# Pacing the second run of first-layer experts beside the first run and the selective scan

## The chip, the cores and the metric

The kernel runs on one core of a Trainium2 chip. The metric is the device time of one execution in microseconds; of several executions the median is given. A core has a matrix engine (TensorE, PE in the rows, its weight loads PEld), a vector engine (VectorE, DVE), an activation engine (ScalarE, ACT), a general engine (GpSimd, POOL) and SyncE (SP), which issues transfers. Each takes its own instructions in program order, and they are tied by semaphores only.

## The reference

Six blocks act in turn on x, of 8 sequences x 512 tokens x 128 features. The first three are the stage that the change touches:

```python
x = x + 0.5 * _L0_ffn_ref(_layernorm(x), W_gate, W1, b1, W2, b2)   # first run of the experts
x = x + _L0_attn_ref(_layernorm(x), ...)                           # a Mamba layer: selective scan
x = x + 0.5 * _L0_ffn_ref(_layernorm(x), ...)                      # second run, same weights
x = x + 0.5 * _L1_ffn_ref(...)                                     # the other three blocks
x = x + _L1_attn_ref(...)
x = x + 0.5 * _L1_ffn_ref(...)

def _L0_ffn_ref(x, W_gate, W1, b1, W2, b2):        # D=128, E=8 experts, H=512, top 2 by a mask
    gate = einsum('bsd,de->bse', x, W_gate)
    kth = top_k(gate, 2)[0][..., -1:]
    mask = softmax(where(gate >= kth, gate, -inf))
    h = relu(einsum('bsd,edh->bseh', x, W1) + b1)
    y = einsum('bseh,ehd->bsed', h, W2) + b2
    return (y * mask[..., None]).mean(axis=-2)

def step(h, inp):                                  # the selective scan, 256 channels x 16 states
    dA = exp(dt_t[..., None] * A)
    h = dA * h + (dt_t * u_t)[..., None] * B_t[:, None, :]
    y = einsum('bdn,bn->bd', h, C_t)
```

Every expert is computed for every token, and the mask weights the results.

## The kernel before

The function `front` computes the first three blocks of all eight sequences as three streams of work that run side by side: `A`, the first run of the experts; `M`, the Mamba layer; `F`, the second run. A sequence must leave `A` before `M` takes it and leave `M` before `F` takes it. The remaining 796 us of the kernel (attention and the experts of the second layer) come behind `front` and are not touched.

**Steps.** A run of the experts has 256 steps: 8 sequences x 8 experts x 4 chunks of 128 hidden features. One step is three matmuls of 512 columns for the up product (lines 118 to 120, the weights and the input being split in a high and a low part), a relu on ACT (line 385, out of one PSUM bank into `hf0`, `hf1` or `hf2`), and the down product for the four token tiles of the step two before (line 354). Behind every fourth step VectorE adds the expert's result, weighted by the mask, onto x (line 413, four instructions). While a sequence is worked on, the norm, the gate and the mask of the next are made in between, at fixed places of its 32 steps (lines 74 to 325). Names that end in `a` belong to the first run, in `b` to the second.

**Scans.** The Mamba layer also has 256 steps, 32 for a sequence (16 states x 2 halves of the channels). One is a decay on ACT (line 767, into `bank4` or `bank5`), a product on POOL (line 777), the scan itself on DVE (line 782), a second product on DVE (line 797) and a sum on POOL (line 808). The projections, the convolution and the softplus of the next sequence stand between them at fixed places (`PREP_*`; lines 612, 620, 626 on PE, 699 to 710 on DVE), and so do the gate and the output projection of the one before (`TAIL_*`; 717 to 728 on PE, 739 and 745 on ACT, 752 and 758 on DVE, 595 and 598 on POOL).

**Slots.** What interleaves the streams is `weave`. It counts slots, and in every slot it takes from each stream so many steps, on each engine alike, as the stream's pace says (one, where it has none). `M` has its scan number 0 in slot 56 (`LM`), one in each slot, and its last in slot 311; its tail lasts until slot 322. `A` begins in slot -12 with 12 steps of preparation and has a pace of its own:

```python
def pace(slot):
    if slot < LM:
        return 1 + (LM - 27 <= slot < LM - 25)
    return 1 + (slot % 3 != 0) if slot < LB else int(slot % 5 != 0)
```

From slot 56 to 109 it takes five steps in three slots, from slot 110 (`LB`) on four in five; its last expert step falls in slot 245. `F` begins in slot 98 with 12 steps of preparation, so that its first expert step falls in slot 110, and takes one step in each slot: its last falls in slot 365. The norms of the block behind `front` are woven in from slot `LN` on, one sequence in five slots (`norms_dve`, `norms_act`).

**Banks.** `HB` and `YB` are two PSUM banks each, for the up and the down products. While both runs are live, each has one of the two; a run that is alone uses both by turns. `first` and `second` decide it by the slot in which the step falls.

Of the kernel before, what the change touches and what calls it, by code (L numbers as in the profile page):

```python
# [17 lines left out]
E = 8  # L18
HID = 512
HC = HID // P  # L20
# [149 lines left out]
def weave(*parts):  # L170

    slot, live = min(part[0] for part in parts), list(parts)
    while live:
        for part in list(live):
            steps = part[2](slot) if len(part) > 2 else 1
            if slot >= part[0] and any(next(part[1], "end") == "end" for _ in range(steps)):
                live.remove(part)
        slot += 1
# [680 lines left out]
def front(nc, S, C, bank, lasting, xin, a, f0, K, w1, sorted_rows):  # L859

    NJ, LM, LB = E * HC, 56, 110
    END = NSEQ * NJ
    LN, norms = LB + END - 40, K["norms"][0]

    def pace(slot):
        if slot < LM:

            return 1 + (LM - 27 <= slot < LM - 25)  # L870
        return 1 + (slot % 3 != 0) if slot < LB else int(slot % 5 != 0)

    with ExitStack() as ctx, ExitStack() as scan_ctx:
        def sb(name, shape, dt=F32):
# [6 lines left out]
        HB, YB, DH, XB, XM = B[0:2], B[2:4], bank[4:6], B[6], B[7]  # L881
# [8 lines left out]


        slots_of_first = [slot for slot in range(-12, 2 * END) for _ in range(pace(slot))]

        def slot_of_first(v):
            return slots_of_first[v + 12]


        def first(k, until):
            return k % 2 if slot_of_first(until) <= LB else 0

        def second(k, since):
            return k % 2 if since >= slot_of_first(END + 2) else 1


        M = mamba(S, C, sb_scan, a, x_of, lambda s: A["done"](s), x_of, lambda s: M["x_read"](s), rows_dram, DH, XM)
# [6 lines left out]
        zero_row, zeroed, cleared = sb("zero_row", [P, NT, WIDE]), S.count("k_zero_row"), S.dma("k_rows_cleared", E * TILES // NT)  # L912
        W = ffn0_up(nc, S, sb, f0)
        A = ffn0(S, C, sb, W, "a", x_of, loaded, x_of, loaded, lambda J: first(J, J + 1), lambda G: first(G, 4 * G + 6), HB, YB, XB)
        F = ffn0(S, C, sb, W, "b", x_of, M["done"], x_of, M["done"], lambda J: second(J, LB + J), lambda G: second(G, LB + 4 * G), HB, YB, XB)

        W["raw"] = F["spent"]
        raw_ld, split = [S.dma(f"k_raw{r}_loaded", (E + 1) * NU // 2) for r in range(4)], K["split"]
# [33 lines left out]
        def split_experts(eng):  # L952
            W["pool"](eng)
            yield

        def pool(eng):
            eng.memset(zero_row[:], 0.0).then_inc(zeroed.sem)
            weave((-12, A["pool"](eng), pace), (0, split_experts(eng)), (LM - NJ, M["pool"](eng)), (LB - 12, F["pool"](eng)))
            eng.wait_ge(*M["done"](NSEQ - 1))
            for i, e in enumerate([E] + list(range(E))):  # L960
                for u in range(NU):
                    k, hi, lo = NU * i + u, K["up_hi"][u][:, e, :], K["up_lo"][u][:, e, :]
                    eng.wait_ge(raw_ld[k % 4].sem, raw_ld[k % 4].at(k // 4))
                    eng.tensor_copy(hi, A["spent"][k % 4]).then_inc(split.sem)
                    eng.wait_ge(split.sem, split.at(k, "hi"))
                    eng.tensor_tensor(lo, A["spent"][k % 4], hi.bitcast(F32), ALU.subtract).then_inc(split.sem)


        def norms_dve(eng):
            for s in range(NSEQ - 1):  # L970
                eng.wait_ge(*F["done"](s))
                norms.mean(eng, s)
                yield
                yield
                norms.scale(eng, s)
                yield
                yield
                yield

        def norms_act(eng):  # L980
            for s in range(NSEQ - 1):
                yield
                norms.root(eng, s)
                for _ in range(4):
                    yield

        def act(eng):
            weave((-12, A["act"](eng), pace), (LM - NJ, M["act"](eng)), (LB - 12, F["act"](eng)), (LN, norms_act(eng)))

        def dve(eng):  # L990
            eng.memset(W["b2"][:], 0.0).then_inc(W["b2_zero"].sem)
            eng.wait_ge(W["b1_T"].sem, W["b1_T"].at(0))
            eng.tensor_copy(W["b1"][:].rearrange("p e c -> p (e c)"), XB.psum[:, 0:E * HC]).then_inc(W["b1_at"].sem)
            weave((-12, A["dve"](eng), pace), (LM - NJ, M["dve"](eng)), (LB - 12, F["dve"](eng)), (LN, norms_dve(eng)))

        def pe(eng):
            eng.wait_ge(W["small"].sem, W["small"].at(0, "b1"))
            eng.transpose(XB.psum[:, 0:E * HC], W["b1_rows"][:], C["ident"][0:E * HC, 0:E * HC]).then_inc(W["b1_T"].sem)
            XB.free = (W["b1_at"].sem, W["b1_at"].at(0))
            weave((-12, A["pe"](eng), pace), (LM - NJ, M["pe"](eng)), (LB - 12, F["pe"](eng)))  # L1000

        with nc.Block() as block:
            block.sync(sync)
# [1138 lines left out]
```

## Time and profile before

| | us |
|---|---|
| median of 3 runs | 1939.84 |
| the runs | 1930.39, 1939.84, 1942.37 |
| profiled execution, its own time | 1927.48 |
| its span, first to last instruction | 1925.7 |
| busy: PE | 1752.5 (91%) |
| busy: DVE | 1250.3 (65%) |
| busy: POOL | 1210.9 (63%) |
| busy: ACT | 1103.0 (57%) |

The span is the time from the first instruction to the last; the 1.8 us to the execution's own time lie around it. Busy times are sums over the whole kernel. Matmuls overlap in the array and their ends are modelled, so that a PE that is busy for 95% of a stretch has hardly anything left to give there. The share of an engine over the whole span says little here, since the streams overlap differently from stage to stage; the windows below cut the stage at the slots at which a pace changes.

### The profile page before, as it was taken

What the parts mean: (1) busy time and instruction counts of PE and PEld (TensorE: products, weight loads), DVE (VectorE), ACT (ScalarE), POOL (GpSimd) and SP (SyncE); (2) the same over time, 40 slices, a digit from 0 to 9 for tenths busy, and PEclk for the clock granted to TensorE, in tenths of its full rate; (3) what the DMA queues carried; (4) which work ended last, traced back from release to release, by engine and by line L of the source; (5) the groups of instructions that cost most, each with busy time, mean ns of one, the idle gap of its engine ahead of it and who ended that gap; (6) DMA issues with size and microseconds to landing.
All of it is one profiled execution on the core that took longest, in us unless ns stands there. A gap on an engine that the chain in (4) does not pass through costs nothing. (4 is left out here: it accounts for less than half of the span.)

```text
span 1925.7 us, 35660 instructions
## 1 busy us (share of the span) xinstructions
PE 1752.5 (91%) x12117; PEld 1506.5 (78%) x12117; DVE 1250.3 (65%) x2930; ACT 1103.0 (57%) x1935; POOL 1210.9 (63%) x1201
## 2 busy tenths in 40 slices
PE   7999898999999999887689989999699999989998
PEld 6878676787877778766477878888599999978886
DVE  2358789778787787978886436433567666656433
ACT  3466665766666766565555554343577767553442
POOL 3228687776877768778895725464656555534664
PEclk9999999999999999999889989999799999989999
DMA  4023332332333223332221401112554354101113
GB/s 145 1 69 113 92 107 87 108 97 86 102 91 109 94 84 108 91 101 78 78 99 55 117 14 44 38 46 67 156 160 127 116 154 137 39 24 35 46 45 108
DMA packets 120638, 166.95 MB, mean 87 GB/s; under 512 B 13878, under 2 KB 55820, under 8 KB 120460
## 3 DMA queue, kind: packets, MB, share of 16 engines
q1 hardware_dynamic: 112716, 147.74, 25.2%
q0 software_dynamic: 7168, 15.87, 2.7%
q8 instruction: 101, 1.65, 0.3%
q10 hardware_dynamic: 576, 1.05, 0.2%
q14 instruction: 77, 0.63, 0.1%
HBM read 114.28 MB, written 50.33 MB: 85 GB/s over the span
## 5 line engine op out<-in xcount | busy, mean ns | idle before, releaser
L777 POOL TENSOR_TENSOR db<-du_m,bt 128x512 f32<-128x512 f32 x256 | 328.5, 1284 | 137.6 <-DVE bank L782 136.7
L782 DVE TENSOR_TENSOR_SCAN bank<-bank,db 128x512 f32<-128x512 f32 x256 | 312.5, 1221 | 20.1 <-ACT bank L767 19.9
L808 POOL TENSOR_TENSOR y_m<-y_m,ph 128x512 f32<-128x512 f32 x240 | 313.4, 1307 | 0.4 <-DVE ph L797 0.4
L767 ACT ACTIVATE bank<-dt_m,a_neg 128x512 f32<-128x512 f32 x256 | 176.2, 688 | 96.6 <-DVE ph L797 90.0
L797 DVE TENSOR_TENSOR ph<-bank,ct 128x512 f32<-128x512 f32 x240 | 165.9, 691 | 11.2 <-POOL y_m L808 3.2
L1241 POOL TENSOR_TENSOR s_a<-s_a,mx_a 128x768 f32<-128x768 f32 x64 | 94.2, 1472 | 88.3 <-DVE mx_a L1349 88.2
L1380 PE MATMUL bank<-vb_a,pT_a 96*128 96x64 f32 x1024 | 121.5, 272 | 0.2 <-DVE o_a L1391 0.2
L1380 PEld LDWEIGHTS bank<-vb_a,pT_a 96*128 96x128 f32 x1024 | 119.4, 192 | 0.3 <-DVE o_a L1391 0.3
L354 PEld LDWEIGHTS bank<-dn,hf2b 128*128 128x128 f32 x680 | 91.3, 196 | 15.4 <-DVE x_all L413 5.7
L354 PEld LDWEIGHTS bank<-dn,hf1b 128*128 128x128 f32 x680 | 89.8, 193 | 11.2 <-DVE x_all L413 2.9
L354 PE MATMUL bank<-dn,hf2b 128*128 128x128 f32 x680 | 92.1, 280 | 6.5 <-DVE x_all L413 4.7
L354 PEld LDWEIGHTS bank<-dn,hf0b 128*128 128x128 f32 x688 | 90.3, 192 | 9.3 <-DVE x_all L413 1.0
L354 PEld LDWEIGHTS bank<-dn,hf2a 128*128 128x128 f32 x680 | 89.6, 193 | 8.5 <-DVE x_all L413 1.3
L354 PEld LDWEIGHTS bank<-dn,hf0a 128*128 128x128 f32 x688 | 90.3, 192 | 7.5
L354 PEld LDWEIGHTS bank<-dn,hf1a 128*128 128x128 f32 x680 | 89.0, 191 | 8.0 <-DVE x_all L413 0.6
L354 PE MATMUL bank<-dn,hf1b 128*128 128x128 f32 x680 | 90.7, 277 | 2.4 <-DVE x_all L413 2.0
L354 PE MATMUL bank<-dn,hf0b 128*128 128x128 f32 x688 | 91.1, 275 | 1.0 <-DVE x_all L413 0.6
L354 PE MATMUL bank<-dn,hf0a 128*128 128x128 f32 x688 | 90.8, 275 | 0.0
L354 PE MATMUL bank<-dn,hf2a 128*128 128x128 f32 x680 | 90.4, 276 | 0.4 <-DVE x_all L413 0.3
L354 PE MATMUL bank<-dn,hf1a 128*128 128x128 f32 x680 | 89.7, 275 | 0.2 <-DVE x_all L413 0.2
L385 ACT ACTIVATE hf1a<-bank,b 128x512 f32<-128x512 f32 x85 | 58.2, 685 | 53.6 <-PE bank L120 53.3
L1311 ACT CAST qd_a<-q_strips_a 32x512 fp32r<-32x512 f32 x128 | 78.7, 615 | 15.6 <-DMA q_strips_a<-q_rows 14.5
(458 smaller groups left out, 4864.9 us busy)
## 6 DMA issues: line engine op xcount, KB each, us to landing
bt<-bc_rows SPq DMA_DIRECT2D x128, 256.0 KB, 3.5
ct<-bc_rows SPq DMA_DIRECT2D x128, 256.0 KB, 3.4
sorted<-zero_row SPq DMA_DIRECT2D x64, 288.0 KB, 3.9
k_strips_a<-k_rows SPq DMA_DIRECT2D x32, 256.0 KB, 3.0
q_strips_a<-q_rows SPq DMA_DIRECT2D x32, 256.0 KB, 3.9
q_rows<-q_hi_a SPq DMA_DIRECT2D x16, 256.0 KB, 3.0
q_rows<-q_lo_a SPq DMA_DIRECT2D x16, 256.0 KB, 3.4
vb_a<-v_rows SPq DMA_DIRECT2D x16, 240.0 KB, 3.9
```

The costliest lines, as they stand in the source:

```text
L354: x = eng.matmul(Y.psum[:, t], hf[r][:, t], W["dn"][:, e, c, :], start=c == 0 and k == 0, stop=c == HC - 1 and k == NT - 1, skip_group_che ...
L385: eng.activation(hf[v % NR][:], HB[hbank(v)].psum[:], ACT.Relu, bias=W["b1"][:, e, c:c + 1]).then_inc(relu.sem)
L767: eng.activation(DH[J % 2][:], dt[s % 2][:, j % NH, :], ACT.Exp, scale=a_neg[:, j % NH, j // NH:j // NH + 1]).then_inc(da_done.sem)
L777: eng.tensor_tensor(db[J % RD][:], du[s % 2][:, j % NH, :], bt[N % RB][:], ALU.mult).then_inc(db_done.sem)
L782: eng.tensor_tensor_scan(DH[J % 2][:], DH[J % 2][:], db[J % RD][:], 0.0, ALU.mult, ALU.add).then_inc(hs_done.sem)
L797: eng.tensor_tensor(out, DH[J % 2][:], ct[N % RB][:], ALU.mult).then_inc(ph_done.sem)
L808: eng.tensor_tensor(y[s % 2][:, j % NH, :], y[s % 2][:, j % NH, :], ph[J % RP][:], ALU.add).then_inc(ys_done.sem)
L1241: eng.tensor_tensor(X[:], X[:], M[:, :, None].to_broadcast([P, UB, KW]), ALU.subtract).then_inc(sub_done.sem)
L1311: x = eng.copy(qd[n % RQ][p, :, r, :], q_strips[n % 2][p, :].rearrange("p (b q) -> p b q", q=QB))
L1380: x = eng.matmul(BO[:, at:at + 2 * GD], pT[u % 2][:, c * BB + j, :], vb[s % 2][:, b:NB + 1:NB - b, g * GD:(g + 1) * GD], start=True, stop= ...
```

## The change

`F` gets a pace. It begins in slot 95 instead of 98, takes four steps in five slots until slot 249 (those slots whose number leaves 2 when divided by 5 are left out, whereas `A` leaves out those that leave 0), then four steps in three slots until slot 326, and one in each slot from there on. The functions that choose its banks ask for the slot by the new table. The norms for the block behind begin in slot 318 instead of 326. No instruction is added, removed or resized in any engine's list but two loads of activation tables on ACT (40 where there were 38); the streams are only dealt out otherwise.

```diff
-    NJ, LM, LB = E * HC, 56, 110
+    NJ, LM, LB, LA, L2 = E * HC, 56, 110, 249, 95
     END = NSEQ * NJ
-    LN, norms = LB + END - 40, K["norms"][0]
+    LN, norms = LB + END - 48, K["norms"][0]
...
+    def pace_second(slot):
+        if slot < LA:
+            return int(slot % 5 != 2)
+        return 1 + (slot % 3 == 0) if slot < LM + END + 14 else 1
...
+        slots_of_second = [slot for slot in range(L2, 2 * END) for _ in range(pace_second(slot))]
+
         def slot_of_first(v):
             return slots_of_first[v + 12]
+
+        def slot_of_second(v):
+            return slots_of_second[v + 12]
...
-        F = ffn0(S, C, sb, W, "b", x_of, M["done"], x_of, M["done"], lambda J: second(J, LB + J), lambda G: second(G, LB + 4 * G), HB, YB, XB)
+        F = ffn0(S, C, sb, W, "b", x_of, M["done"], x_of, M["done"], lambda J: second(J, slot_of_second(J)), lambda G: second(G, slot_of_second(4 * G)), HB, YB, XB)
...
-            weave((-12, A["pe"](eng), pace), (LM - NJ, M["pe"](eng)), (LB - 12, F["pe"](eng)))
+            weave((-12, A["pe"](eng), pace), (LM - NJ, M["pe"](eng)), (L2, F["pe"](eng), pace_second))
```

The same edit of the last line stands in the functions of the other engines. Counted by the two tables, the steps of `F` fall thus (those of `A` and the scans stay where they are):

| slots | scans | steps of `A` | steps of `F` before | steps of `F` now |
|---|---|---|---|---|
| 110 to 245 | 136 | 108 | 136 | 109 |
| 246 to 311 | 66 | 0 | 66 | 86 |
| 312 and on | 0 | 0 | 54 | 61 |

How it looks on ACT, where a slot begins with its decay (line 767) and the relus of the two runs follow. This is the stage with both runs live, a part of it without preparations, before:

```order
L767 ACTIVATE bank5<-dt1_m,a_neg 128x512
L385 ACTIVATE hf1b<-bank1,b1 128x512
L385 ACTIVATE hf2a<-bank0,b1 128x512
L767 ACTIVATE bank4<-dt1_m,a_neg 128x512
L385 ACTIVATE hf2b<-bank1,b1 128x512
L385 ACTIVATE hf0a<-bank0,b1 128x512
L767 ACTIVATE bank5<-dt1_m,a_neg 128x512
L385 ACTIVATE hf0b<-bank1,b1 128x512
L385 ACTIVATE hf1a<-bank0,b1 128x512
```

And now, ACT at such a part of the same stage:

```order
L767 ACTIVATE bank5<-dt1_m,a_neg 128x512
L385 ACTIVATE hf1b<-bank1,b1 128x512
L385 ACTIVATE hf2a<-bank0,b1 128x512
L767 ACTIVATE bank4<-dt1_m,a_neg 128x512
L385 ACTIVATE hf0a<-bank0,b1 128x512
L767 ACTIVATE bank5<-dt1_m,a_neg 128x512
L385 ACTIVATE hf2b<-bank1,b1 128x512
L385 ACTIVATE hf1a<-bank0,b1 128x512
L767 ACTIVATE bank4<-dt1_m,a_neg 128x512
L385 ACTIVATE hf0b<-bank1,b1 128x512
L767 ACTIVATE bank5<-dt1_m,a_neg 128x512
```

Where every slot but the fifth held two steps, two slots in five now hold one, once of the one run and once of the other.

Behind the end of the first run, ACT before has one relu behind each decay:

```order
L767 ACTIVATE bank4<-dt0_m,a_neg 128x512
L385 ACTIVATE hf1b<-bank1,b1 128x512
L767 ACTIVATE bank5<-dt0_m,a_neg 128x512
L655 ACTIVATE du1_m<-u1_m 128x512
L385 ACTIVATE hf2b<-bank0,b1 128x512
L767 ACTIVATE bank4<-dt0_m,a_neg 128x512
L385 ACTIVATE hf0b<-bank1,b1 128x512
```

ACT at the corresponding place now:

```order
L767 ACTIVATE bank4<-dt0_m,a_neg 128x512
L385 ACTIVATE hf0b<-bank0,b1 128x512
L767 ACTIVATE bank5<-dt0_m,a_neg 128x512
L655 ACTIVATE du1_m<-u1_m 128x512
L385 ACTIVATE hf1b<-bank1,b1 128x512
L385 ACTIVATE hf2b<-bank0,b1 128x512
L767 ACTIVATE bank4<-dt0_m,a_neg 128x512
```

One slot in three holds a second step of the same run, which takes the other of the two banks.

The third place is ACT in slots 317 to 320, where the last sequence leaves the Mamba layer (`gT` is the gelu, `sg` the two halves of the gate) and which now also hold the first root of the norms (`sd_k`). Before:

```order
L739 ACT_TABLE_LOAD
L739 ACTIVATE gT<-bank7 128x512
L385 ACTIVATE hf0b<-bank1,b1 128x512
L745 ACTIVATE sg<-bank7 128x256
L385 ACTIVATE hf1b<-bank0,b1 128x512
L385 ACTIVATE hf2b<-bank1,b1 128x512
L745 ACTIVATE sg<-bank7 128x256
```

And now:

```order
L739 ACT_TABLE_LOAD
L739 ACTIVATE gT<-bank7 128x512
L385 ACTIVATE hf1b<-bank0,b1 128x512
L745 ACTIVATE sg<-bank7 128x256
L385 ACTIVATE hf2b<-bank1,b1 128x512
L385 ACTIVATE hf0b<-bank0,b1 128x512
L385 ACTIVATE hf1b<-bank1,b1 128x512
L84 ACT_TABLE_LOAD
L84 ACTIVATE sd_k<-mv_k,eps 128x4
L745 ACT_TABLE_LOAD
L745 ACTIVATE sg<-bank7 128x256
```

The root of the norms has come between the two halves of the last gate, with a table load ahead of it and one behind it.

## Rows read from the trace of the kernel before

**Rows 1.** The page: engines over the whole span, and the granted clock in 40 slices.
```profile
PE 1752.5 (91%) x12117; PEld 1506.5 (78%) x12117; DVE 1250.3 (65%) x2930; ACT 1103.0 (57%) x1935; POOL 1210.9 (63%) x1201
PEclk9999999999999999999889989999799999989999
```

**Rows 2.** Windows: slots 110 to 245, 246 to 311, and from 312 to the end of `front`.
```profile
core 0: us, PE busy (x) PEld busy (x) DVE busy (x) ACT busy (x) POOL busy (x), PEclk, DMA share, GB/s
325.30:839.80 514.50, 480.63 (x2919) 395.37 (x2920) 407.77 (x791) 343.98 (x561) 383.27 (x336) 0.99 0.31 97
839.80:1033.80 194.00, 152.28 (x836) 121.40 (x835) 170.61 (x280) 112.40 (x181) 176.41 (x151) 0.90 0.27 82
1033.80:1129.80 96.00, 94.11 (x628) 83.19 (x626) 36.17 (x164) 46.78 (x75) 40.20 (x45) 1.00 0.25 75
```

**Rows 3.** The count of scans and relus in the first two of these windows, by line.
```profile
L782 DVE TENSOR_TENSOR_SCAN bank<-bank,db x136: 1197/1221/1232, 325.3 to 837.9; 128x512 f32<-128x512 f32 x136
...
L385 ACT ACTIVATE hf0b<-bank,b x46: 667/687/691, 325.9 to 838.6; 128x512 f32<-128x512 f32 x46
...
L385 ACT ACTIVATE hf0a<-bank,b x36: 668/687/699, 336.1 to 834.2; 128x512 f32<-128x512 f32 x36
...
L782 DVE TENSOR_TENSOR_SCAN bank<-bank,db x66: 1198/1221/1232, 839.8 to 1031.8; 128x512 f32<-128x512 f32 x66
```

**Rows 4.** Timeline near the end of `front`: a step on PE, an addition on DVE.
```profile
1118.33 0.48 PE L118 MATMUL bank<-xT_hi1b,up_hi 128*128 128x512 f32 x1
1118.65 0.40 PE L119 MATMUL bank<-xT_lo1b,up_hi 128*128 128x512 f32 x1
1118.89 0.40 PE L120 MATMUL bank<-xT_hi1b,up_lo 128*128 128x512 f32 x1
1119.12 1.05 PE L354 MATMUL bank<-dn,hf0b 128*128 128x128 f32 x8
1119.93 0.48 PE L118 MATMUL bank<-xT_hi1b,up_hi 128*128 128x512 f32 x1
...
1123.40 1.13 DVE L413 SCALAR_TENSOR_TENSOR x_all<-bank,mk1b,x_all 128x128 f32<-128x128 f32 x4 [5.26 <-PE bank L354]
```

**Rows 5.** Windows of slots 72 to 87 and 88 to 103, first run alone, columns as above.
```profile
182.60:242.80 60.20, 51.73 (x323) 42.90 (x323) 49.17 (x93) 39.78 (x66) 41.76 (x36) 1.00 0.28 86
242.80:303.30 60.50, 55.20 (x341) 46.11 (x340) 51.07 (x111) 40.33 (x71) 51.92 (x51) 1.00 0.34 103
```

**Rows 6.** Waits in slots 110 to 245.
```profile
POOL db L777 <- DVE bank L782: 96.5, 49, 6.4
DVE x_all L413 <- PE bank L354: 69.9, 36, 6.5
```

**Rows 7.** Windows that cut slots 246 to 311 in four, columns as above.
```profile
839.80:893.90 54.10, 43.12 (x246) 34.17 (x245) 47.66 (x87) 33.08 (x55) 51.99 (x49) 0.97 0.30 87
893.90:950.80 56.90, 40.41 (x214) 30.25 (x213) 47.50 (x74) 31.85 (x52) 42.06 (x34) 0.85 0.24 72
950.80:996.10 45.30, 35.19 (x186) 28.25 (x186) 39.02 (x64) 27.06 (x44) 45.06 (x39) 0.88 0.29 98
996.10:1033.80 37.70, 33.55 (x197) 28.73 (x196) 36.42 (x59) 20.41 (x33) 37.30 (x32) 0.92 0.23 72
```

**Rows 8.** Waits in slots 246 to 311.
```profile
ACT bank L767 <- DVE ph L797: 47.5, 38, 4.6
POOL db L777 <- DVE bank L782: 11.3, 7, 4.1
...
PE bank L620 <- DVE u_m L706: 7.7, 1, 7.7
...
PE bank L612 <- DVE u_m L702: 6.9, 1, 6.9
PE bank L354 <- DVE x_all L413: 6.5, 2, 4.7
```

**Rows 9.** Groups by line in slots 104 to 247: count, busy us, mean ns, idle before.
```profile
L702 DVE SCALAR_TENSOR_TENSOR u_m<-bank,conv_w,u_m 128x511 f32<-128x511 f32 (+2 forms) x30 | 22.4, 745 | 0.7
```

**Rows 10.** Line 752 on DVE from slot 104 to 247, and from slot 248 on.
```profile
L752 DVE SCALAR_TENSOR_TENSOR y_m<-u_m,cols,y_m x8: 737/745/1266, 369.0 to 735.5; 128x512 f32<-128x512 f32 x8
...
L752 DVE SCALAR_TENSOR_TENSOR y_m<-u_m,cols,y_m x4: 1229/1486/1762, 850.5 to 957.0; 128x512 f32<-128x512 f32 x4
```

**Rows 11.** Table loads ahead of the norms' roots, over the whole span.
```profile
L84 ACT ACT_TABLE_LOAD x2 | 2.6, 1283 | 0.0
```

More of the change, by code:

```diff
@@ L957, in pool @@
             eng.memset(zero_row[:], 0.0).then_inc(zeroed.sem)
-            weave((-12, A["pool"](eng), pace), (0, split_experts(eng)), (LM - NJ, M["pool"](eng)), (LB - 12, F["pool"](eng)))
+            weave((-12, A["pool"](eng), pace), (0, split_experts(eng)), (LM - NJ, M["pool"](eng)), (L2, F["pool"](eng), pace_second))
             eng.wait_ge(*M["done"](NSEQ - 1))
@@ L987, in act @@
         def act(eng):
-            weave((-12, A["act"](eng), pace), (LM - NJ, M["act"](eng)), (LB - 12, F["act"](eng)), (LN, norms_act(eng)))
+            weave((-12, A["act"](eng), pace), (LM - NJ, M["act"](eng)), (L2, F["act"](eng), pace_second), (LN, norms_act(eng)))
         def dve(eng):
@@ L993, in dve @@
             eng.tensor_copy(W["b1"][:].rearrange("p e c -> p (e c)"), XB.psum[:, 0:E * HC]).then_inc(W["b1_at"].sem)
-            weave((-12, A["dve"](eng), pace), (LM - NJ, M["dve"](eng)), (LB - 12, F["dve"](eng)), (LN, norms_dve(eng)))
+            weave((-12, A["dve"](eng), pace), (LM - NJ, M["dve"](eng)), (L2, F["dve"](eng), pace_second), (LN, norms_dve(eng)))
         def pe(eng):
```

## The prediction

> **What bounds the kernel now.** I began with the page, where PE is busy for 91% of the span and no other engine for over 65% [rows 1]. That would make any rearrangement idle, since no work is removed. But the row of the granted clock dips in slices 20 to 24, some 920 to 1150 us, and a clock that is not granted means a PE that had too little to do. So I cut the front stage at the slots where the paces change [rows 2]. Three stages show. In slots 110 to 245, with both runs and the scans, PE is busy for 480.6 of 514.5 us (93%), DVE for 79%, POOL for 74%: PE bounds it, at 514.5 / 136 = 3.78 us a slot. The waits say the same: POOL stands 96.5 us before its product, waiting for the scan, and DVE stands 69.9 us before it adds an expert's result, waiting for the down product [rows 6]. In slots 246 to 311, with one run and the scans, PE is busy for 152.3 of 194.0 us at a granted clock of 0.90, DVE for 88% and POOL for 91%: there POOL and DVE bound it, at 2.94 us a slot, and the waits turn round: PE waits for DVE, 7.7 and 6.9 us at a stretch, ahead of the Mamba layer's projections [rows 8]. From slot 312 on PE is busy for 94.1 of 96.0 us. PE idles 33.9, 41.7 and 1.9 us in the three. This imbalance is what the change can work on: expert steps leave the first stage, where they cost PE time, and are to enter the second, where PE idles.
>
> **The price of a step.** At the end of front a step of a run that is alone starts 1.60 us behind the one before (1119.93 - 1118.33) [rows 4]. The counts are in the code's table and agree with the trace: 136 scans, three relu groups of about 46 and three of 36 in the first stage, that is 136 steps of the second run and 108 of the first; 66 scans in the second [rows 3].
>
> **Slots 110 to 245.** 27 steps leave: 27 x 1.60 = 43 us of PE work, 437.4 us of busy time being left. How much of that the time follows depends on PE's idle time, 0.25 us a slot now (33.9 / 136). It won't stay: a thinner PE meets the dense places of DVE, three convolution taps of 0.75 us beside a scan [rows 9], more often first. The nearest rows with fewer steps are slots 72 to 103, where the first run alone takes five steps in three slots (1.67, against 1.6 to come and 1.79 now): PE is busy for 106.9 of 120.7 us, idle 13.8 / 32 = 0.43 us a slot [rows 5]. There the double steps are all of one run and each waits for the relu before it, which two alternating runs don't, so I take 0.35, the middle of the two. Idle time grows by 0.10 x 136 = 14 us, and the stage gets 43 - 14 = **29 us shorter**. Ends: 43 us, if idle time doesn't grow; 15 us, if it rises to 0.45. DVE's load is no obstacle: it was 407.8 us and loses 27 / 4 additions of 1.13 us [rows 4], about 400, against 485 us that the stage would then last.
>
> **Slots 246 to 311.** 20 steps enter: 32 us of PE work. Some comes free. A clock of 0.90 over 194 us is, with its two levels of 2.4 and 1.2 GHz, 39 us at the lower one, in which PE does at most 39 / 2 = 19 us less. The low clock follows the stretches where PE waited for DVE (0.85 in the window with the two long waits, 0.97 in the fullest one) [rows 7]. With a third more steps in each slot I expect most of it back, 12 us. PE then has 152.3 + 32 - 12 = 172 us to do. With the idle time of 0.35 to 0.4 us a slot, 25 us, this stage lasts 197 us: **3 us longer**. DVE, at 170.6 + 20 / 4 x 1.13 = 176 us, and POOL, at 176.4, also fit. By quarter: the second had 47.5 us of DVE in 56.9 and should shrink; the last, without a next sequence to prepare, had PE at 33.6 of 37.7 us and must grow by a few us. Ends: 172 + 0.25 x 66 = 189, 5 us shorter; or 25 us longer, if three quarters of the 32 us lie bare (below).
>
> **From slot 312 on.** 7 steps more on an engine that is 98% busy: 7 x 1.60 = **11 us longer**. Nothing hides this. The clock is full there and the Mamba layer's tail needs PE for a few instructions only, so both ends lie within 1 us.
>
> **What moves with it.** Starting in slot 95 keeps the first expert step in slot 110; the statistics of the first sequence, at step -10, fall in slot 98, the slot in which the Mamba layer releases it, where before there were two slots between. If DVE waits there, it is once and for less than a slot, and the margin grows by eight slots with each sequence. I count nothing. The norms eight slots earlier put a root between the halves of the last gate, and two more table loads of 1.28 us on ACT [rows 11]. ACT is busy for under half of that stage, but the second half of the gate, and by it the release of the last sequence, comes later by the 2.6 us, and a relu queued behind the loads may hold PE: I take **1 us**, between 0 (the last sequence is asked for in slot 326 and not 324, so the release has time) and 3. The weight loads and splits for the next block begin with that release; POOL stands idle at the end of front even now, so they stay covered.
>
> **The sum.** -29 + 3 + 11 + 1 = -14 us on the profiled execution's 1927.5, and the same is taken off the median, which lies 12 us higher: 1939.84 - 14 = 1926. A difference of under 1% (19 us) is about what runs that spread from 1930 to 1942 can't tell from none.
>
> **A rule against it.** Line 752, with two inputs from SBUF, takes 745 ns at the median while POOL is busy for 74% and 1486 ns where POOL is at 91% [rows 2, 10]. Shorter slots make POOL denser in the first stage, 383 of 485 us or 79%. Eight to ten such instructions stand there, and if they all went from 745 to 1486 ns that would be 10 x 0.74 = 7 us of DVE, of which a part would be PE idle time; it lies within the ends above. The Trainium skill ("GPSIMD Engine Reference", Key points) has the cause: GpSimd shares its SBUF interfaces with VectorE and contends with its instructions that have two SBUF inputs. By that rule all of it would come, and the sum would be -7 instead of -14.
>
> **Rivals.**
> *Full relief.* PE's idle time is the Mamba layer's chain and not the pace's, and doesn't grow; the clock comes back whole. For: the 1.79-step stage idles less than the one with 1.67 steps only where the latter is a single run. Against: the long waits for DVE where PE has little to do [rows 8]. Then -43 - 5 + 11 + 1 = -36, or 1904; half of the way there is -25, 1915.
> *No room beside the scans.* PE waits in both stages until DVE's dense places are past, whatever it has to do: idle 0.45 in the first (-15), +6 in the second, +12 behind: +3, or 1943. For: slots 72 to 87 take 3.76 us with PE busy for only 86% [rows 5], as long as slots with 1.79 steps.
> *Double steps lie bare*, the case on the slower side. In one slot of three PE now has two steps of one run, 3.2 us, before DVE can add the expert's result (line 413) and go on to its next scan, and POOL waits for that scan. A slot there lasts 2.94 us, so that such a slot exceeds it by itself, and the two single slots between may not give it back since ACT's decay runs at most one scan ahead [rows 8]. If 25 of the 32 us are bare and the first stage gives only 15: -15 + 25 + 11 + 1 = +22, 1962. It decides against the change from the point where more than two thirds of the second stage's added work shows in its time and the first stage gives less than 20 us. Against: POOL may run three products ahead, and PE is one step ahead of the relus with two banks.
>
> **How the numbers follow.** The forecast, -14 with a range of its own from -19 to -4 (1921 to 1936), gets 0.43; full relief, -19 to -36, gets 0.37; no room, within 1%, gets 0.11; bare double steps get 0.09. Faster by over 1% is full relief, 0.37; within 1% are the forecast and no room, 0.54; slower is the last case, 0.09. The range goes from full relief's end, 1904, to somewhat above no room's 1943, at 1946, and leaves out the last case and a sliver below.
>
> **What would show it.** In the changed profile slots 110 to 245 should take 485 us or so (3.57 a slot) with PE at 90%; if they take 500, the first term failed. Slots 246 to 311 should take about 197 us, PE's granted clock there 0.96 or more; a wait of DVE at line 413 for PE that grows from next to nothing to 20 us or more there would show bare double steps. From slot 312 to the end of front it should be 107 us. Everything behind front should keep its 796 us; if the next block starts later because its weights aren't split, or if its clock differs, the prediction would be wrong for a reason outside this sum. It would also be wrong if the waits for DVE's convolution (lines 702 and 706) grow by more than 0.1 us a slot in the first stage.

## The result, and the profile after

The changed kernel takes 1953.56 us at the median of 4 runs (1953.35 to 1955.6), the one before 1938.99 us (1930.39 to 1942.37): a ratio of 1.0084, with a 95% interval of 1.0051 to 1.0118. It is slower by 14.6 us, under 1% but beyond what the runs spread. The profiled execution took 1955.6 us with a span of 1953.9 us, 28 us over the profiled one of before; that one had lain 12 us under its own median.

The same three windows as in [rows 2], cut at slots 110, 246, 312 and the end of front, give for the changed kernel (busy time of each engine, granted clock, share and rate of the transfers):

```profile
core 0: us, PE busy (x) PEld busy (x) DVE busy (x) ACT busy (x) POOL busy (x), PEclk, DMA share, GB/s
326.90:830.90 504.00, 447.30 (x2599) 359.42 (x2600) 403.27 (x741) 320.98 (x526) 382.26 (x333) 0.97 0.32 99
830.90:1043.70 212.80, 180.28 (x1075) 150.35 (x1073) 181.33 (x326) 128.07 (x210) 177.01 (x153) 0.94 0.24 75
1043.70:1153.10 109.40, 107.50 (x712) 94.55 (x710) 40.42 (x169) 54.35 (x85) 40.17 (x45) 1.00 0.22 66
```

The first stage is 10.5 us shorter (514.5 to 504.0), the second 18.8 us longer (194.0 to 212.8), the third 13.4 us longer (96.0 to 109.4). Up to slot 110 it is 1.6 us later (326.9 against 325.3). Together front is 23.3 us longer. The other 5 us lie behind front, where the change touches nothing (windows of the changed kernel, of the one before, and of the one before in a later execution, from the end of front to the end):

```profile
1153.10:1953.90 800.80, 744.33 (x5955) 668.40 (x5955) 431.47 (x1232) 412.07 (x804) 426.21 (x471) 0.96 0.27 81
```

```profile
1129.80:1925.70 795.90, 739.22 (x5955) 663.93 (x5955) 431.35 (x1232) 412.10 (x804) 426.84 (x471) 0.97 0.27 82
```

```profile
1142.50:1963.10 820.60, 747.00 (x5955) 666.86 (x5955) 435.18 (x1232) 413.87 (x804) 427.03 (x471) 0.96 0.27 79
```

The same kernel took 795.9 us there once and 820.6 us another time. Whole spans of single executions are therefore no measure of this change; the stage times below are.

In the first stage PE now idles 504.0 - 447.3 = 56.7 us, 0.42 us a slot, where it idled 33.9. Its busy time fell by 33.3 us only, although 27 steps of 1.60 us had left. The waits there (who waited for whom, us in total, times, longest), in excerpts of one view:

```profile
POOL db L777 <- DVE bank L782: 98.4, 41, 7.6
ACT bank L767 <- DVE ph L797: 50.6, 36, 4.4
DVE x_all L413 <- PE bank L354: 50.2, 38, 6.1
...
DVE bank L782 <- ACT bank L767: 20.7, 12, 3.8
...
PE bank L354 <- DVE x_all L413: 10.0, 15, 3.4
PE bank L620 <- DVE u_m L706: 9.2, 5, 2.3
...
PE bank L612 <- DVE u_m L702: 6.8, 3, 2.4
```

POOL and DVE still wait as in [rows 6], DVE for PE 20 us less. In their place DVE's scan waits 20.7 us for ACT's decay, and PE waits 10.0 us for the additions that free its bank. PE's waits for the convolution (lines 702 and 706) are 16.0 us in all. The same four waits before the change:

```profile
DVE bank L782 <- ACT bank L767: 10.3, 7, 3.5
...
PE bank L620 <- DVE u_m L706: 8.5, 5, 2.7
...
PE bank L612 <- DVE u_m L702: 4.5, 4, 1.6
...
PE bank L354 <- DVE x_all L413: 1.3, 4, 0.6
```

In the second stage, against [rows 8], the changed kernel shows:

```profile
ACT bank L767 <- DVE ph L797: 36.9, 24, 3.6
POOL db L777 <- DVE bank L782: 24.8, 13, 5.1
DVE x_all L413 <- PE bank L354: 18.0, 9, 4.8
...
PE bank L114 <- ACT xnb L104: 7.6, 2, 4.1
ACT xnb L104 <- POOL nmb L100: 6.9, 2, 3.7
```

PE's two long waits for the Mamba layer's convolution (7.7 and 6.9 us) are gone from the head of the list. DVE's wait for the down product, 5.8 us in all before the change, is 18.0 us, and a chain that runs from POOL's norm over ACT's scaling to PE's transpose holds PE twice, for 3.5 to 4.1 us each time, where before it held it once, for 4.4 us. By quarter the stage took 57.7, 53.5, 56.3 and 45.3 us; in [rows 7] it was 54.1, 56.9, 45.3 and 37.7. The quarter in which PE had waited most got shorter and the last two, which hold the preparations of sequences 5 and 6 of the second run, carry most of the loss. The first quarter, 3.6 us longer, now holds one more: by the table of slots the preparation of sequence 4 falls in slots 254 to 259, where it fell in 228 to 235 before. The statistics of DVE in slots 246 to 311, four for a sequence, show three preparations where there were two; the first line is from the kernel before, the second from the changed one:

```profile
L74 DVE BATCH_NORM_STATS2 statsb<-x_all 128x6 f32<-128x128 f32 x8 | 1.7, 278 | 0.0
```

```profile
L74 DVE BATCH_NORM_STATS2 statsb<-x_all 128x6 f32<-128x128 f32 x12 | 2.6, 277 | 0.0
```

### The profile page after: what moved, and what is told of

Same layout as the page of the kernel before. It is cut to its first block and busy times, and to the rows that moved or that the text cites. A ratio compares the mean times of both kernels' runs of the same rounds, so it can differ in the third digit from the quotient of the medians.

```text
span 1953.9 us, 35662 instructions
## 1 busy us (share of the span) xinstructions
PE 1766.2 (90%) x12117; PEld 1515.7 (78%) x12117; DVE 1261.7 (65%) x2930; ACT 1103.4 (56%) x1937; POOL 1209.8 (62%) x1201
## 5 line engine op out<-in xcount | busy, mean ns | idle before, releaser
L1379 ACT COPY pT_a<-bank 96x512 f32<-96x512 f32 x128 | 68.0, 580 | 35.5 <-PE bank L1372 35.5
L1346 PE MATMUL bank<-kT_a,qd_a 128*128 128x96 f32 x512 | 73.6, 289 | 14.5 <-ACT qd_a L1322 12.0
```

The source lines that it names most:

```text
L1346: x = eng.matmul(BS[c][:, j * KW:(j + 1) * KW], qd[n % RQ][:, b, :, :].rearrange("p r q -> p (r q)"), kT[n % RQ][:, b * QB:b * QB + KW], s ...
L1379: eng.copy(pT[u % 2][:, c * BB:(c + 1) * BB, :].rearrange("p b q -> p (b q)"), BT[c][0:KW, :]).then_inc(pT_done.sem)
```

## The experiments

All stage times below are from the windows of each kernel's trace, cut at the same slots; I call them stage 1 (slots 110 to 245), stage 2 (246 to 311) and stage 3 (312 to the end of front).

| kernel | stage 1 | stage 2 | stage 3 | ratio to the one before, 95% interval |
|---|---|---|---|---|
| before | 514.5 | 194.0 | 96.0 | |
| before_again | 517.4 | 196.8 | 96.1 | one execution |
| changed | 504.0 | 212.8 | 109.4 | 1.0084 (1.0051 to 1.0118) |
| norms_back | 500.0 | 213.2 | 110.5 | 1.0108 (1.0067 to 1.0149) |
| slow_only | 501.1 | 191.5 | 143.8 | 1.0153 (1.0117 to 1.0189) |
| mild | 505.0 | 194.2 | 104.0 | 1.0015 (0.9995 to 1.0035) |
| full_catch_up | 505.4 | 199.2 | 98.3 | 0.9990 (0.9965 to 1.0015) |
| before_light | 506.3 | 194.1 | 85.8 | 0.9880 (0.9846 to 0.9914) |
| dve_light | 507.7 | 189.8 | 95.5 | 0.9976 (0.9944 to 1.0007) |
| both_light | 493.0 | 188.6 | 84.3 | 0.9798 (0.9770 to 0.9825) |
| after_light | 493.5 | 211.2 | 97.3 | 0.9992 (0.9966 to 1.0018) |
| after_heavy_2 | 515.2 | 215.6 | 124.0 | 1.0271 (1.0207 to 1.0336) |
| late_add | 500.6 | 206.7 | 110.5 | 1.0058 (1.0038 to 1.0078) |
| early_norm | 501.0 | 208.9 | 109.0 | 1.0068 (1.0042 to 1.0094) |
| late_and_early | 500.9 | 204.2 | 109.1 | 1.0025 (1.0004 to 1.0046) |
| catch_up_eased | 505.4 | 201.2 | 98.2 | 0.9976 (0.9959 to 0.9993) |

### How far a stage time can be trusted: before_again

The kernel before, unchanged.

> The kernel before, once more, for its stage times on another chip: they stand as 514.5, 194.0 and 96.1 us in one trace only. If the stages are what the comparison takes them for, they come back within 3 us each, and what differs between executions lies behind front, where the traces so far range from 796 to 826 us.

The stages came back within 2.9, 2.8 and 0.1 us, and the difference of 25 us lay behind front. Likewise the five kernels whose stage 1 is that of the changed one (norms_back, slow_only, late_add, early_norm, late_and_early) have 500.0 to 501.1 us there. The changed kernel's own 504.0 is the outlier, so that the change's effect on stage 1 is 514.5 or 517.4 less about 501: 14 to 16 us, and 10.5 in the one pair of profiles. Differences in a stage below 3 us mean nothing.

### Is it the norms? norms_back

```diff
-    LN, norms = LB + END - 48, K["norms"][0]
+    LN, norms = LB + END - 40, K["norms"][0]
```

> The changed kernel with the norms for the next block woven in from slot 326 again, as before the change. Load theory (the loss is made by the paces in slots 110 to 311): the last part of front gets 1 to 3 us shorter, the kernel stays 12 to 14 us over the one before. Tail theory (the root between the halves of the last gate delays the last sequence's release and all behind it): 8 us or more come back, and the kernel is within 6 us of the one before.

Stage 3 took 110.5 us where it had 109.4, and the ratio stayed, 1.0108 against 1.0084 with overlapping intervals. The root between the halves of the last gate and its table loads cost nothing that can be measured: the tail theory fell, and so did the 1 to 3 us of the other.

### The slower pace alone: slow_only

```diff
-        if slot < LA:
-            return int(slot % 5 != 2)
-        return 1 + (slot % 3 == 0) if slot < LM + END + 14 else 1
+        return int(slot % 5 != 2) if slot < LA else 1
...
-    LN, norms = LB + END - 48, K["norms"][0]
+    LN, norms = LB + END - 28, K["norms"][0]
```

> Only the slower pace: four steps in five slots until slot 249, then one in each; norms 12 slots later than before so that they still find their sequences done. 27 steps are left over for the part behind slot 312. Load theory: slots 110 to 245 take 504 us as in the changed kernel, slots 246 to 311 go back to 190 to 196 us, the rest grows by 27 x 1.60 = 43 us: +30 us against the kernel before, ratio 1.016. If the second stage stays above 205 us with single steps, it isn't the double steps but the shifted phase of the preparations that costs there.

Stage 2 went back to 191.5 us. Both stage 2s follow a stage 1 in which the second run had fallen behind by the same 27 steps, so what costs there comes with the catching up and not with the lag as such. The places of the preparations aren't the same in the two, though: slow_only has two of them in stage 2, the changed kernel three. Against the changed kernel, 20 steps more in stage 2 cost 212.8 - 191.5 = 21.3 us, and the same 20 behind slot 312 cost 143.8 - 109.4 = 34.4 us, 1.7 each. Catching up beside the scans is worth having; falling behind isn't.

### Half the shift: mild, and full_catch_up

```diff
-    NJ, LM, LB, LA, L2 = E * HC, 56, 110, 249, 95
+    NJ, LM, LB, LA, L2 = E * HC, 56, 110, 249, 97      # full_catch_up: LA = 246
...
-    LN, norms = LB + END - 48, K["norms"][0]
+    LN, norms = LB + END - 40, K["norms"][0]
...
-            return int(slot % 5 != 2)
-        return 1 + (slot % 3 == 0) if slot < LM + END + 14 else 1
+            return int(slot % 10 != 2)
+        return 1 + (slot % 6 == 0) if slot < LM + END + 14 else 1      # full_catch_up: slot % 5
```

> Half the shift: the second run leaves out one slot in ten instead of one in five until slot 249, then takes seven steps in six slots, and begins in slot 97; norms from slot 326. 14 steps leave slots 110 to 245, 3 more than before are left at slot 312. Load theory (each step taken away gives 0.4 us in the first stage, each put in costs 0.9 us in the second and 1.6 us behind it): -5 + 10 + 5 = +9 us against the kernel before, ratio about 1.004. Phase theory (the loss depends on where the second run's preparations meet those of the Mamba layer, not on how many steps are moved): no such proportion, anything from -8 to +20 us.

Stage 1 fell by 9.5 us, nearly as far as with the whole shift (10.5 to 14) for half the steps. Stage 2 took 194.2 us with some ten steps more than before, that is, nothing, and 8 us came behind. The proportion that the load theory assumed doesn't hold: the first ten steps go in free, the next ten cost 19 us. In time the kernel is not told apart from the one before. The preparation of sequence 4 begins in slot 241 here and falls into stage 2 with its latter part only, so how much of the next 19 us is that preparation and how much the steps isn't separated.

> The half shift of the earlier run, but caught up in full before the scans end: one slot in ten left out until slot 245, then six steps in five slots until slot 326, so that the second run stands at step 201 in slot 312 (before: 202; in the half shift: 198). Free-room theory (the first 10 or so added steps find room beside the scans at the clock they bring back, and what was lost was only the steps left over behind): slots 110 to 245 take 505 us, slots 246 to 311 194 to 198, from 312 on 96 to 98: -4 to -9 us against the kernel before, ratio 0.996. Load theory as first put (0.9 us for each added step): +12 us in the second stage, ratio 1.001 or more.

The steps that mild left over behind the scans were put beside them. Stage 3 went from 104.0 to 98.3 us, stage 2 from 194.2 to 199.2. The stages sum to 802.9 us against 804.5 before, and the ratio is 0.9990, no difference. Three more steps cost 5 us in stage 2, which suggests that the free room was used up; 5 us is not far above the scatter of 3.

### What bounds the first stage: before_light, dve_light, both_light

In the first, the second run's up product has two matmuls:

```diff
-                three(eng, H.psum[:], W["up_hi"][:, e, h], W["up_lo"][:, e, h], xT_hi[q][:], xT_lo[q][:]).then_inc(up_done.sem)
+                if tag == "b":
+                    eng.matmul(H.psum[:], W["up_hi"][:, e, h], xT_hi[q][:], start=True, stop=False)
+                    eng.matmul(H.psum[:], W["up_lo"][:, e, h], xT_hi[q][:], start=False, stop=True).then_inc(up_done.sem)
...
```

> The kernel before, with two matmuls instead of three in the up product of the second run (the one with the low part of the input is left out, so that part of the computation is missing); paces and order untouched. It takes 0.24 us of PE work off each of its steps: 33 us in slots 110 to 245, 16 in slots 246 to 311, 13 behind. Load theory (the first stage is held by the coupling of engines as much as by PE's load): the first stage gives 10 to 16 us, the second 0 to 5, the rest 13: 25 to 32 us in all. Phase theory (PE's load does bound the first stage, and the new order wasted it): the first stage gives 28 us or more, the whole 43 or more.

33 us of PE work out of stage 1 gave 8.2 us (10.9 against before_again), 16 us out of stage 2 gave nothing, and 13 us behind gave 10.2. The first number is at or under the lower end of the load theory's 10 to 16 and far from the phase theory's 28. This is the run that contradicts the reading on which the prediction stood: PE was 93% busy, and yet a microsecond of its work was worth a quarter to a third of one. The windows of its first two stages:

```profile
330.80:837.10 506.30, 458.00 (x2784) 375.93 (x2785) 407.04 (x791) 342.10 (x561) 383.35 (x336) 0.97 0.31 98
837.10:1031.20 194.10, 138.58 (x772) 109.58 (x772) 172.17 (x280) 112.37 (x182) 175.20 (x150) 0.90 0.25 82
```

In stage 1 PE's idle time grew from 33.9 to 48.3 us, and its busy time fell by 22.6 and not 33 us. A part of the rest is clock: by the trace's records PE was at the lower of its two levels (1.2 and 2.4 GHz) for 27 us of this stage where it had been for 10, and if work takes twice as long there, that is up to 9 us of busy time more. The thinner PE idled more and was granted less here; both_light below idled more too (42.7 us) and was granted 0.99, so the one doesn't simply follow from the other.

In the second, VectorE adds one token tile of four:

```diff
-                    for k in range(NT):
+                    for k in range(1 if tag == "b" else NT):
                         x = eng.scalar_tensor_tensor(acc_at(s)[:, k, :], Y[:, k * P:(k + 1) * P], ...)
```

> The kernel before, in which the second run adds only one of four token tiles of each expert's result (three quarters of these additions are missing). It takes 0.8 us of VectorE work off every fourth step: 27 us in slots 110 to 245, 13 in slots 246 to 311. Coupling theory (the first stage stands near a floor set by VectorE, ACT and POOL passing work to each other, just below PE's own load): 4 to 12 us come out of the first stage. PE theory (PE's load bounds it): under 4 us.

> Both cuts on the kernel before: two up matmuls, and one of four additions in the second run. The up cut alone made the first stage 8 us shorter for 33 us of PE work. Coupling theory: with VectorE lighter too the first stage falls by more than the sum of the two alone, 25 us or more under the kernel before's 514. Floor theory (the floor is POOL's or a latency's, which neither cut touches): it stays at 500 us or more.

27 us of DVE work, of which 22 came off its busy time, gave 6.8 us of stage 1, as the coupling theory had it, in an engine that was 79% busy. Both together gave 21.5 us for 60 us of work, more than the 15.0 of the two alone, but less than the 25 that the coupling theory wanted. Against before_again it is 24.4 and 20.6, so the excess of 4 to 6.5 us is hardly above the scatter, and a part of it may be clock (0.99 in both_light, 0.97 in before_light). The floor theory, at 500 us, is excluded by 7 us. So stage 1 has no single bound: relieving PE or DVE alone is worth a quarter to a third of what is taken off. That they pass the wait around, with ACT's decay in between, is read from the waits; no run made ACT or POOL lighter.

### The same cut, and its opposite, on the changed kernel: after_light, after_heavy_2

after_light is the first cut made to the changed kernel; after_heavy_2 issues the first up matmul twice:

```diff
+                if tag == "b":
+                    eng.matmul(H.psum[:], W["up_hi"][:, e, h], xT_hi[q][:], start=True, stop=True)
                 three(eng, H.psum[:], W["up_hi"][:, e, h], W["up_lo"][:, e, h], xT_hi[q][:], xT_lo[q][:]).then_inc(up_done.sem)
```

> The changed kernel with two matmuls instead of three in the up product of the second run (the low part of the input is left out: that part of the computation is missing). It takes 0.24 us off each of its steps: 26 us in slots 110 to 245, 21 in slots 246 to 311, 15 behind. PE theory (the second stage of the changed kernel is over PE's capacity): slots 246 to 311 fall from 213 us by 15 us or more. Chain theory (two steps of one run in a slot make VectorE and ACT wait for PE, and the chain of the next sequence's preparation is squeezed into fewer slots): they fall by under 8 us. In the first stage 0 to 6 us under both.

> The changed kernel with the first up matmul of the second run issued twice into the same bank (the second overwrites the first, the result is the same). It puts 0.24 us of PE work on each of its steps: 26 us in slots 110 to 245, 21 in 246 to 311, 15 behind; the pace stays. Coupling theory (in the first stage a microsecond of PE work counts for a quarter to a third): that stage gets 5 to 10 us longer than its 500 to 504. PE theory: 20 us or more longer. Behind slot 312 it is 13 to 15 us under both.

In stage 2 the matter is plain: 21 us less of PE work gave 1.6 us and 21 us more cost 2.8. PE's load doesn't bound the second stage at all, and the chain theory had its number. In stage 1 I was off twice: the cut gave 7 us of its 26 against the 501 that this stage usually takes (10.5 against 504.0), where 0 to 6 were expected, and the extra work cost 11 to 14 us, neither the 5 to 10 of the one theory nor the 20 of the other. The slope is 0.3 to 0.4 us for a microsecond downward and 0.4 to 0.5 upward, by which of the two values of the stage it is taken from. The extra work also kept the clock: in stage 2 it was granted at 0.98.

```profile
328.50:843.70 515.20, 469.47 (x2704) 377.52 (x2705) 401.45 (x740) 322.97 (x525) 381.91 (x333) 0.98 0.31 97
843.70:1059.30 215.60, 193.45 (x1153) 162.87 (x1152) 181.72 (x326) 128.11 (x209) 177.36 (x153) 0.98 0.24 74
```

With the clock at 0.98 stage 2 was still 215.6 us long, so what was left of the low clock there (0.94 in the changed kernel) is hardly what it waits for.

### What costs in the second stage: late_add, early_norm, late_and_early

```diff
-            J = v - LEAD - late
+            J = v - LEAD - (tag == "b" and v >= 112)                  # late_add
-            if 0 <= J < END:
+            if 0 <= J < END and not (tag == "b" and v == 112):
...
-    PREP_DVE = (22, 22, 25, 27, ...)    PREP_POOL = (23,)
+    PREP_DVE = (20, 20, 25, 27, ...)    PREP_POOL = (21,)            # early_norm, sequences 5 and 6 of the second run
```

> The changed kernel, in which the second run's additions on VectorE (line 413) fall one step later than before from its step 112 on (slot 250); nothing else is touched. Addition theory (in a slot with two steps VectorE stands at the addition until both down products are made, and the next scan stands behind it): slots 246 to 311 fall from 213 us to 203 or less. Preparation theory (what costs there is the chain of norm, scale, transpose and split for the next sequence, which has fewer slots now): they stay at 208 or more.

> The changed kernel, in which sequences 5 and 6 of the second run get their statistics and the scales on POOL two steps earlier (places 20 and 21 instead of 22 and 23), so that ACT's scaling at place 24 has POOL's result in time. Preparation theory: the two waits of PE for ACT of 4.1 and 3.5 us at these places vanish and slots 246 to 311 fall by 6 us or more. Addition theory: they fall by under 3 us.

> The changed kernel with both: the additions one step later from step 112 on and the norms of sequences 5 and 6 two steps earlier. If both theories hold a part, the gains of the two alone add up in slots 246 to 311 to within 2 us. If the stage is bound by the number of steps after all, it stays at 205 us or more whatever is eased.

Neither theory had its number alone, and both hold a part. Stage 2 fell by 6.1 us with the additions late, by 3.9 with the norms early, and by 8.6 with both; alone they sum to 10.0. Of the 6.1 us one came back behind slot 312 (110.5 us), into which one addition moved. The waits went as they should. DVE's wait for the down product, 18.0 us in the changed kernel, is 1.6 in late_add, though DVE's scan now waits 9.0 us for the decay:

```profile
DVE bank L782 <- ACT bank L767: 9.0, 7, 2.5
...
DVE x_all L413 <- PE bank L354: 1.6, 2, 1.2
```

and PE's wait for the scaled input, 7.6 us, is 0.5 in early_norm:

```profile
PE bank L114 <- ACT xnb L104: 0.5, 2, 0.3
```

Easing both makes the changed kernel better (ratio 1.0025 against 1.0084, the intervals being 1.0004 to 1.0046 and 1.0051 to 1.0118), but stage 2 is still 204.2 us against 194.0 to 196.8. Of the 19 us that it had grown by, 9 went with these two waits; the last 7 to 10 stay open. One candidate is the third preparation. DVE's busy time there rose from 170.6 to 181.3 us: 6.5 us of it are additions (line 413, 19.3 to 25.8 us), and the other 4 us fit the preparation of sequence 4, which also stands on PE, ACT and POOL. No run kept it out of the stage while the steps came in.

### The best of it: catch_up_eased

full_catch_up with both easings, the additions from step 124 on.

> The half shift with full catch-up (slots 246 to 311 took 199 us there, 5 more than in the kernel before), and both easings: additions one step later from step 124 on, norms of sequences 5 and 6 two steps earlier. If what the added steps cost is these two waits, the second stage falls to 190 to 194 us and the kernel comes to -6 to -11 us against the one before, ratio 0.994 to 0.997; if not, it stays at 199 and the ratio at 0.999.

The ratio is 0.9976 with an interval of 0.9959 to 0.9993, the only complete kernel here whose interval lies below 1, by 0.2%. Its reason isn't shown: stage 2 took 201.2 us and not the 190 to 194 expected, no less than the 199.2 without the easings. The two waits had little to give: in full_catch_up DVE waited 8.6 us in stage 2 at line 413 and PE 4.0 for the scaled input, near the 5.8 and 4.4 of the kernel before. And the late additions brought a wait of their own, where they begin: PE stood once for 10.7 us before a down product, for the addition that frees its bank, where the longest such wait in full_catch_up was 6.5 us (this kernel's edit moves line 354 to 361 and line 413 to 420).

```profile
PE bank L361 <- DVE x_all L420: 10.7, 1, 10.7
```

## Why the prediction was wrong

The forecast was 1926 us, -14, in a range of 1904 to 1946; it came to 1953.6, +14.6. By the prediction's own steps, with the sizes of the pair of profiles:

| step | predicted | measured |
|---|---|---|
| slots 110 to 245 | -29 (ends -43, -15) | -10.5 (about -15 against the stage's usual 501) |
| slots 246 to 311 | +3 (ends -5, +25) | +18.8 |
| from slot 312 on | +11 | +13.4, with the next |
| norms and table loads | +1 | not measurable (stage 3 was 110.5 us in norms_back, without the earlier norms) |
| start in slot 95 | 0 | front is 1.6 us later at slot 110, where the kernel before alone differed by 6.9 |

**The step that failed is the first one's conversion of work into time**: "PE bounds it", read off 93% busy time, and then idle time growing by 0.10 us a slot. It grew by 0.17, to 0.42, next to the 0.43 of the two windows in [rows 5], which I had halved away with an argument on double steps. Besides, I priced a step at 1.60 us of busy time, but PE was granted less, 0.97 where it had been 0.99: of 43 us of work that left only 33 came off the busy time. before_light shows the same without any change of pace, and a price: 0.25 to 0.33 us of stage 1 for a microsecond of PE work, or 11 to 14 us for 43. The change also takes relus, additions and one preparation out of the stage, so this price needn't be the whole of it.

The reason that I gave for the idle time, the dense places of DVE's convolution, was not the one either. PE's waits for lines 702 and 706 grew from 13.0 to 16.0 us, 0.02 us a slot; of the 22.8 us that idle time grew by, the largest part that the waits show, 8.7 us, is for the additions of line 413 that free the bank of the down products.

**The second term was mis-sized, and its mechanism was named as a rival.** The clock came back in part, from 0.90 to 0.94 and not to 0.96: by the records of the trace 37.5 us at the lower level became 23.9, which is 7 us of work and not the 12 that I had counted. The quarter with the long waits got shorter, as said. PE had 180 us to do and idled 32.5 us, not 172 and 25, and DVE had 181 and not 176: the sum counted the steps that enter and left out the third preparation. But capacity wasn't the question: after_light and after_heavy_2 moved PE's load by 21 us either way and the stage by 1.6 and 2.8. What grew were waits that come from two steps of one run in one slot: 18.0 us of DVE at line 413, near the 20 us that the prediction had set as the mark of bare double steps, and PE's 7.6 us behind the norm, which I hadn't seen. Line 413's wait was worth 6 us of stage time, that behind the norm 4; for the other 7 to 10 us no cause is shown.

The rival *double steps lie bare* came nearest, at 1962 against 1953.6: first stage -15 against -10.5 to -15, second +25 against +18.8, +11 against +13.4 behind. It was given 0.09. Its price of 25 us was too high, since half of the added steps do find room (mild), and its condition for a loss, over two thirds of the 32 us showing, wasn't met (18.8 us, or 59%): the rest of the loss came with the small gain of the first stage and the third term. *No room beside the scans* had the first stage right and the second too low, +6. *Full relief* wanted PE's idle time in the first stage not to grow; it grew from 33.9 to 56.7 us.

**The rule of the Trainium skill that was weighed** spoke against the change. In the changed kernel line 752 takes 784 ns at the median in stage 1 where it took 745, a twentieth of the way to the 1486 of [rows 10], but line 310, also with two inputs from SBUF, went from 194 to 706 ns at the median in the second run:

```profile
L310 DVE TENSOR_TENSOR selb<-lgb,topb x8: 191/706/1304, 307.0 to 1091.6; 128x32 f32<-128x32 f32 x8
```

That GpSimd shares its SBUF interfaces with VectorE and contends with such instructions ("GPSIMD Engine Reference", Key points, in the Trainium skill) is thus borne out by the instructions of the gate, which the change moved beside POOL's products, and not by those that I had counted. In sum the eight instances of line 310 took 5.9 us where they had taken 4.1, those of line 313 5.9 against 2.9 and of line 316 4.7 against 2.5: 7 us of DVE over the whole of front, while the eight of line 752 in stage 1 took 0.6 us more.

## What to carry to other kernels

An engine that is 93% busy needn't be the bound where two others are busy for 79% and 74% and all three hand work to each other in program order. Take a known amount of its work away and see what the stage gives back, before moving work on the strength of its busy share: here it was a quarter to a third. Work moved into a stage with room enters free only as far as it fits between the hand-overs there (ten steps in 66 slots); beyond that the price is set by what queues behind a doubled slot, and easing those waits (a consumer one step later, a producer two steps earlier) was worth more here than the balance of the load. Count also what is tied to the steps that move: here a whole preparation went with them into the stage that was to have room. A nearby stage that already runs at the load one is moving to is the best witness for its idle time, and shouldn't be argued away.

## What the runs showed of the hardware that was not expected

- PE's granted clock falls in a stage that stays busy. In the changed kernel's first stage it fell to the lower of its two levels (1.2 and 2.4 GHz) eight times, for 27 us in all, in the kernel before three times, for 10 us. At each fall stood one wait of PE of 1.4 to 3.4 us (1.7 to 4.2 before the change), but not every such wait was followed by a fall: there were 22 of 1.4 us or more, and 11 before the change. The timeline of PE has one of them, a wait of 2.32 us for a convolution. Ahead of it lines 119 and 120 start 0.24 us apart, behind it 0.42 us:

```profile
428.49 0.40 PE L119 MATMUL bank<-xT_lo1a,up_hi 128*128 128x512 f32 x1
428.73 0.39 PE L120 MATMUL bank<-xT_hi1a,up_lo 128*128 128x512 f32 x1
428.96 1.05 PE L354 MATMUL bank<-dn,hf1a 128*128 128x128 f32 x8
432.34 1.62 PE L612 MATMUL bank<-hT,w_in 128*128 128x512 f32 x2 [2.32 <-DVE u_m L702]
432.97 1.41 PE L118 MATMUL bank<-xT_hi0b,up_hi 128*128 128x512 f32 x1
434.19 0.63 PE L119 MATMUL bank<-xT_lo0b,up_hi 128*128 128x512 f32 x1
434.61 0.63 PE L120 MATMUL bank<-xT_hi0b,up_lo 128*128 128x512 f32 x1
```

  In before_light and in the changed kernel PE had more such waits and paid for them twice: 17 us more at the lower level took up to 9 us (an estimate, work at half the rate) of the 33 or 43 us that had been saved. The relation is loose: both_light had 14 such waits, against 15 in before_light, and was at the lower level for 10 us only. It would follow that the waits that the change lengthens cost more than their length; that wasn't tried by itself.
- The part behind front took from 795.9 to 820.6 us for the same kernel, at almost equal busy times of PE (739 and 747 us). On a difference of 1% in front it weighs more than the change, and only windows of the stage show the difference.
- A short instruction of VectorE with two inputs from SBUF that starts while POOL works on a product or a sum ends only when POOL's instruction ends. Line 310 takes 0.19 us with POOL idle; here it starts 0.06 us behind a product of POOL, at 900.55, and ends at 903.01, behind that product and the sum that followed it:

```profile
900.49 1.26 POOL L777 TENSOR_TENSOR db<-du_m,bt 128x512 f32<-128x512 f32 x1
900.55 2.46 DVE L310 TENSOR_TENSOR selb<-lgb,topb 128x32 f32<-128x32 f32 x1
901.70 1.26 POOL L808 TENSOR_TENSOR y_m<-y_m,ph 128x512 f32<-128x512 f32 x1
...
903.05 0.19 DVE L313 TENSOR_TENSOR lgb<-lgb,topb 128x32 f32<-128x32 f32 x1
```

  Of the 48 instances of lines 310, 313 and 316 of the second run in the traces of the kernel before and of the changed one, the 22 beside which POOL was idle took 0.18 to 0.19 us, and 25 of the other 26 ended within 0.1 us behind an instruction of POOL.
